# A fused attention and expert layer: the order of work in the first slot of each batch

## The reference

```
q, k, v = x @ w_q, x @ w_k, x @ w_v          # x: 512 x 256, layer-normed
q, k    = rope(q), rope(k)
p       = softmax((q @ k.T) / 128 - 1e30 * mask)
out    += (p @ v) @ w_o                      # summed over the 8 heads
```

## Time and profile before

| | |
|---|---|
| median of 3 runs | 1266.8 us (1266.45 to 1269.58) |
| the profiled execution's own time | 1270.0 us |
| its span in the trace | 1268.2 us |
| PE busy | 1125.1 us, 89% of the span |
| PE weight loads busy | 984.5 us, 78% |
| DVE busy | 836.5 us, 66% |
| POOL busy | 821.9 us, 65% |
| ACT busy | 692.3 us, 55% |

### The profile page before, as it was taken

The page is one execution under the profiler, slowest core; times in us unless marked ns, Lnnn a source line. Parts: engine busy times, 40 slices in busy tenths (PEclk is TensorE's granted clock), DMA queues, the critical chain, the costliest instruction groups (busy, mean ns, idle before and its releaser), DMA issues. The chain is left out here.

```text
span 1268.2 us, 20248 instructions
## 1 busy us (share of the span) xinstructions
PE 1125.1 (89%) x6999; PEld 984.5 (78%) x6999; DVE 836.5 (66%) x2108; ACT 692.3 (55%) x1432; POOL 821.9 (65%) x848
## 2 busy tenths in 40 slices
PE   3899999999999999999999985017999999999995
PEld 2788888878878888888888852015999999999994
DVE  4777787787887877877877743775564555554421
ACT  4566656666656666666576631103554554654641
POOL 3797887887887987978977810014664654754425
PEclk9999999999999999999999997557999999999998
DMA  5000100100100100101100013004433523523213
GB/s 186 1 18 1 38 30 1 42 26 1 43 25 25 39 5 34 34 1 38 30 1 34 18 34 108 1 7 129 118 69 72 129 54 85 130 38 98 33 18 34
DMA packets 42209, 58.08 MB, mean 46 GB/s; under 512 B 8896, under 2 KB 34944, under 8 KB 41984
## 3 DMA queue, kind: packets, MB, share of 16 engines
q0 software_dynamic: 13824, 21.24, 9.3%
q1 hardware_dynamic: 28288, 35.58, 8.4%
HBM read 35.71 MB, written 16.91 MB: 41 GB/s over the span
## 5 line engine op out<-in xcount | busy, mean ns | idle before, releaser
L1149 DVE TENSOR_TENSOR hT_lo<-hid,hT_hi 128x512 fp32r<-128x512 f32 x128 | 89.0, 696 | 178.8 <-ACT hT_hi L1267 178.8
L198 POOL TENSOR_SCALAR prob<-prob,row_inv 128x512 f32<-128x512 f32 (+3 forms) x256 | 135.4, 541 | 69.2 <-DVE row_inv L418 67.5
L1265 ACT ACTIVATE hid<-up,b_e 128x512 f32<-128x512 f32 x128 | 88.1, 688 | 154.9 <-PE up L1332 143.7
L272 ACT ACTIVATE prob<-prob,row_min 128x512 f32<-128x512 f32 (+3 forms) x256 | 142.4, 556 | 40.2 <-DVE row_min L411 39.3
L973 POOL DMA_INDIRECT got<-routed_rows,tokens x64 | 85.8, 1341 | 106.1 <-DVE tokens L1143 86.6
L354 DVE TENSOR_TENSOR pT_lo<-bank,pT_hi 128x384 fp32r<-128x384 f32 (+1 forms) x192 | 114.4, 596 | 42.4 <-ACT pT_hi L254 42.4
L984 POOL TENSOR_SCALAR y<-y,gate 128x256 f32<-128x256 f32 x64 | 34.0, 543 | 134.8 <-issue 134.0
L993 POOL DMA_INDIRECT out<-y,tokens x64 | 104.8, 1638 | 17.2 <-issue 14.8
L411 DVE CUSTOM_DVE_ANT_0 prob<-bank,mask_row 128x512 f32<-128x512 f32 (+3 forms) x256 | 114.2, 483 | 0.0
L206 POOL TENSOR_TENSOR q_sin<-q_sin,rope_t 128x512 f32<-128x512 f32 x64 | 82.5, 1289 | 44.7 <-ACT q_sin L296 43.2
L600 PE MATMUL bank<-ident,prob 128*128 128x128 f32 x640 | 101.7, 273 | 5.6 <-POOL prob L198 5.6
(11 more groups left out here) (195 smaller groups left out, 3828.3 us busy)
## 6 DMA issues: line engine op xcount, KB each, us to landing
raw<-in_w SPq DMA_DIRECT2D x16, 1024.0 KB, 8.0
emb_res<-emb SPq DMA_DIRECT2D x8, 512.0 KB, 3.7
out<-h SPq DMA_DIRECT2D x8, 512.0 KB, 2.9
routed_rows<-x SPq DMA_DIRECT2D x8, 512.0 KB, 3.2
x<-in_wq SPq DMA_DIRECT2D x1, 1024.0 KB, 5.2
x<-in_wk SPq DMA_DIRECT2D x1, 1024.0 KB, 4.9
x<-in_wv SPq DMA_DIRECT2D x1, 1024.0 KB, 7.1
x<-in_wo SPq DMA_DIRECT2D x1, 1024.0 KB, 10.1
```

The source lines that it names most:

```text
L198: nc.gpsimd.tensor_scalar(pr, pr, row_inv[:, h % 2, k:k + 1], 1.0, ALU.mult, ALU.mult).then_inc(s["norm_done"], 1)
L272: nc.scalar.activation(pr, pr, ACT.Exp, bias=row_min[:, h % 2, k:k + 1], scale=-1.0, accum_out=row_sum[:, h % 2, k:k + 1]).then_inc(s["exp ...
L1149: nc.vector.tensor_tensor(out, in_, hi.bitcast(F32), ALU.subtract)\
L1265: nc.scalar.activation(hid[:, t % 2, :], up_ps[t % 2][:], ACT.Gelu, bias=bias)
```

## The change

Three things are done, in all engines that the work passes through.

In slot 0 PE runs `weigh(b, h-3)` ahead of the two projections; in all other slots it stays behind them. ACT follows in slot 0 with `oT_hi` ahead of the two `swap` copies, and DVE with the one-column reciprocal and `oT_lo` ahead of `rope_q` and `turn_k`. In slots with `h` of 1 or more, the q projection waits for the first value tile of the slot before instead of the last. That differs for `h` = 1 only, since only slot 0 makes two tiles. POOL's and SP's queues have the same rows as before.

```diff
--- before.py
+++ after.py
@@ -314,12 +314,14 @@
                 for h in slots:
                     n = b * H + h
                     live = ok(h) and h < H
-                    if live:
+                    if live and h != 0:
                         swap(b, h)
                     if ok(h - 3):
                         after(act, "o_done", n - 3 + 1)
                         after(act, "out_done", n - 3)
                         hi_of(oT[0][:], o_ps[:], "o_hi")
+                    if live and h == 0:
+                        swap(b, h)
                     if ok(h - 2):
                         t_high(b, h - 2, 0)
                     if live:
@@ -479,16 +481,19 @@
                 for h in slots:
                     n = b * H + h
                     live = ok(h) and h < H
-                    if live:
+                    if live and h != 0:
                         rope_q(b, h)
                     if ok(h - 2):
                         after(dve, "exp_done", TB * (n - 2) + 4)
                         inverse(b, h - 2, 3, 4)
-                    if live:
+                    if live and h != 0:
                         turn_k(b, h)
                     if ok(h - 3):
                         after(dve, "o_hi", n - 3 + 1)
                         low_of(oT[1][:], o_ps[:], oT[0][:], "o_lo")
+                    if live and h == 0:
+                        rope_q(b, h)
+                        turn_k(b, h)
                     if ok(h - 2):
                         t_low(b, h - 2, 0)
                     if ok(h - 1):
@@ -563,7 +568,7 @@
                 if h == 0:
                     after(pe, "xt_lo", KT * (b + 1))
                 elif x == "q":
-                    after(pe, "v_lo", 2 * TB * b + V_SLOT[h - 1][-1] + 1)
+                    after(pe, "v_lo", 2 * TB * b + V_SLOT[h - 1][0] + 1)
                 elif h == 1:
                     after(pe, "v_lo", 2 * TB * b + 2)
                 else:
@@ -643,6 +648,8 @@
                 for h in slots:
                     n = b * H + h
                     live = ok(h) and h < H
+                    if ok(h - 3) and h == 0:
+                        weigh(b, h - 3)
                     if live:
                         if isinstance(b, int) and b == 0 and h == 0:
                             pe.wait_ge(s["w_lo"], 1)
@@ -650,7 +657,7 @@
                         if isinstance(b, int) and b == 0 and h == 0:
                             pe.wait_ge(s["w_lo"], 2)
                         project(b, h, "k")
-                    if ok(h - 3):
+                    if ok(h - 3) and h != 0:
                         weigh(b, h - 3)
                     if ok(h - 2):
                         after(pe, "norm_done", TB * (n - 2) + 2)
```

## The result

The changed kernel takes 1288.84 us (median of 6 runs, 1286.22 to 1289.23) against 1266.76 us (6 runs): a ratio of 1.0164, with a 95% interval of 1.0154 to 1.0175. It is slower by 22 us, 7 us more than the sum of the prediction, and inside its range by 0.16 us. The profiled executions are 1270.0 us before and 1288.92 after, 18.9 us apart.

What follows compares the result with a forecast made beforehand. PE, busy 89% of the span, was taken as the bound. Wait 10.4 plus clock 6.2 less first batch 1.2 gave +15.4 us: 1285.4 us on the profiled execution, 1282 on the median, range 1274 to 1289.

Steps and rivals of the forecast that it cites:

- The wait: PE, slot 0 at seven batch starts: weighted sum waits 2.16 us for pT_lo instead of 0.68 for xT_lo, costing 10.4 us.
- Fill 2: Weighted sum in slot 0: pT_lo of fill 2 ends at 197.13 us, before its three matmuls need it at 197.71.
- Nothing won back in the slot: PE has no gap up to slot 1's q projection at 206.84, so nothing absorbs the later start of the sum.
- the margin of 1.0 us before slot 1: First v_lo of slot 0 ends at most at 207.3 us; slot 1's q projection wants it at 208.3.
- the moves on ACT and DVE at 0: oT_hi and oT_lo first in slot 0 on ACT and DVE delay nobody; costed at 0.
- The first batch: Slot 1's q projection waits for one value tile only: gain taken as 1.2 us, with 0.6 and 2.2 as ends.
- The clock: Low TensorE clock behind the 2.16 us waits: 1.56 us per stretch, bounds none to seven of seven (0 to 10.9 us).
- I take 4, so 6.2 us: Number of the seven batch starts assumed to be followed by a low-clock stretch, and their total cost.
- 3 to 5 of seven: Case of the wait plus low clock at some batch starts: 1281 to 1284 us, taken as 1282; chance 0.45.
- the one with a chance of 0.15: Rival: low clock at nearly all seven batch starts, up to 1287.5 us; chance 0.15.
- would have given 1276 us: Rival: the wait alone, clock always spared at the batch starts, 1266.8 + 9.2 = 1276 us; chance 0.25.

Runs made afterwards that it cites:

- fill 1 first: Changed kernel with fill 1 of pT_hi (ACT) and pT_lo (DVE) ahead of the xT copies in slot 7: 1272.5 us, ratio 1.0040 to the kernel before.
- PE's order alone: Changed kernel with ACT and DVE back in the order of before, weighted sum still first on PE: 1287.63 us, ratio 1.0158.
- the edit alone: Kernel before with only the q projection of head 1 waiting for one value tile: 1267.4 us against 1267.85, ratio 0.9994.
- work in the wait: Changed kernel with head 0's q projection done once more (six matmuls) ahead of the weighted sum in slot 0: 1277.15 us, ratio 1.0070.
- The five traces: Traces with waits of about 2 us at seven batch starts: the changed kernel's and four experiments'; low clock behind seven, six, six, six and two starts.
- the longer batch: Changed kernel with the k projection done twice in slot 3 of each batch: 1289.98 us, ratio 1.0172.

## Why the prediction was right, and where its size was off

- The wait. The step "the operand of the step put first is ready 1.48 us after the operand of the step that it displaces" held to 0.01 us at the third batch start, and the wait of 2.16 us that follows from it stood at seven places of seven. Slot 8 of the last batch had shown a wait of this kind in the trace of before.
- Fill 2 was met, as reckoned. The experiment with fill 1 first shows that this margin hung on the lateness of fill 1.
- Nothing won back in the slot, and the margin of 1.0 us before slot 1 kept: 1.1 us in the trace after, and the moves on ACT and DVE at 0 (PE's order alone: 1.0158 against 1.0164).
- The first batch: 1.2 us taken, 1.63 us measured in the trace at 38.73. One low stretch went with the shorter wait, one stayed. The time of the edit alone couldn't be told from none.
- The clock. The cost of one stretch, taken as 1.56 us, held: 1.55 in the slot, and over the batch 1.45 by the sum above or 1.50 to 1.57 by the batches with the same wait and no low stretch (90.70 with PE's order alone, 90.63 with work in the wait). The mis-sized term is the number of stretches: "I take 4, so 6.2 us". It was seven, 7 x 1.45 = 10.2 us in the profiled execution, or up to 11.0. The likeliest case was therefore not 3 to 5 of seven but the one with a chance of 0.15, and its bound of 1287.5 us was passed too. The rows of before held both facts (the length of the wait and the two low stretches), but I treated seven starts as seven draws. The five traces don't look like draws: seven, six, six, six and two of seven, with what follows a start tied to the length of the batch.
- Luck in the number. The sum was 1282 us, the measured time some 7 us more: 4.0 us are the three stretches not counted, 0.4 less the first batch, and 3.2 us stand in the last point. That 1288.84 still lies in a range up to 1289 isn't owed to a term of the sum.
- The Trainium skill, TensorE: Matmul & The Clock Gate, says in "The HAM clock gate" that the monitor's window runs free of the program; that the same wait of 2.16 us was followed by the low clock at two starts of the longer batch and by full rate at five agrees with it. Its rule in "HAM oscillation", that only gaps longer than a window do harm, would have given 1276 us, and the measured 1288.84 is against it.
- The 3.2 us between 18.9 and 22.1 stand between the profiled execution of before and its own median. The granted clocks point to low stretches: the profiled execution had a mean granted clock of 0.955, and among the 29 executions of the kernel before that ran beside the experiments, the six at 0.955 and 0.956 took 1268.5 to 1269.8 us and the five at 0.959 took 1265.5 to 1267.4. Where those stretches lie, in the first batch (30.21 and 40.36 in the earlier trace rows) or elsewhere, no trace shows. The changed kernel's own runs split the same way: 1286.2 and 1286.6 us at 0.950, the other four 1288.8 to 1289.2 at 0.948 and 0.949. That would be a start or two that were spared, but no trace of these two was taken.

## What to carry to other kernels

Before a step is put ahead to cover a wait, look up when its own operands are ready: here those came later than the one waited for, since on the helping engines they stood behind it. The order has to be changed on all engines that feed the step, or on none. And a wait of about 2 us on a busy TensorE should be priced with the clock, 1.5 us beside each wait here. In a loop its rounds aren't independent: five traces had seven, six, six, six and two low rounds of seven, so forecast with nearly all and with few, and not with the middle.

## What was not expected of the hardware

Adding 1.39 us of matmuls to a wait made the kernel 11.7 us faster, as the clock was then kept at seven starts; adding the same 1.39 us elsewhere in each batch, 11.1 us in all, cost 1.1 us against the changed kernel (1289.98 against 1288.84 us), in the main as only two of seven starts fell to the low clock. Waits of 1.10 us (fill 1 first) and 1.43 us (first batch) were followed by full rate; waits of 1.89 to 1.90 us were followed by the low clock at six starts of seven, and waits of 2.16 us by either.
